# Tokens of a core pair split at 1152 instead of interleaved, with the first core's attention run two blocks ahead

## The reference, cut to what matters

```python
# B, T, C = 4, 2048, 2048; 16 heads of 128; hidden width 8192
xn = layernorm(x)
q, k, v = split(xn @ w_atten.T);  q, k = rope(q), rope(k)
att = softmax(where(causal, q @ k.T / sqrt(128), -inf))
s = (att @ v) @ w_proj.T
h = silu(xn @ w_gate) * (xn @ w_up)
h = keep_largest_2_of_4(h)          # by absolute value, in groups of four of the hidden width
g = silu(h @ w_down)
out = x + s * g
```

## Time and profile before

| | us |
|---|---|
| median of three runs | 2398.1 |
| the profiled execution, whole | 2320.1 |
| its span on the slowest core (5) | 2318.6 |
| spans of the eight cores | 2313.8 to 2318.6 |
| PE busy | 2233.9 (96%) |
| VectorE busy | 996.6 (43%) |
| ScalarE busy | 635.7 (27%) |
| the span in five stages, by PE's first and last matmuls | 126.0, 777.3, 110.5, 857.7, 447.1 |

### The profile page before, as it was taken

The page is one execution under the profiler, slowest core; times in us unless marked ns, Lnnn a source line. Parts: engine busy times, 40 slices in busy tenths (PEclk is TensorE's granted clock), DMA queues, the critical chain, the costliest instruction groups (busy, mean ns, idle before and its releaser), DMA issues.

```text
span 2318.6 us, 35747 instructions; the slowest of 8 cores (2313.8 to 2318.6 us)
## 1 busy us (share of the span) xinstructions
PE 2233.9 (96%) x12736; PEld 1181.9 (51%) x12736; DVE 996.6 (43%) x1441; ACT 635.7 (27%) x1082; POOL 137.5 (6%) x260
## 2 busy tenths in 40 slices
PE   4789999999999988999999999999999999999999
PEld 3547566675766744444444444444444444444444
DVE  5566867768677673004444443333333331000111
ACT  4624344444434434122222222222222200000000
POOL 0000000000000000000000000000000000000000
PEclk8999999999999999999999999999999999999999
DMA  9342322223122143754434344444554479766661
GB/s 268 109 79 47 61 40 45 57 44 66 38 46 56 33 79 74 156 111 80 83 74 73 73 80 83 90 94 91 97 101 94 91 168 238 157 127 132 132 138 44
DMA packets 82732, 217.38 MB, mean 94 GB/s; under 512 B 9984, under 2 KB 30592, under 8 KB 80000
## 3 DMA queue, kind: packets, MB, share of 16 engines
q0 software_dynamic: 36864, 134.23, 33.7%
q1 hardware_dynamic: 44576, 79.94, 11.0%
q10 hardware_dynamic: 1120, 0.92, 0.1%
HBM read 311.53 MB, written 25.17 MB: 145 GB/s over the span
## 4 chain that ended last, share of the span: by engine, by line
PE 82%; DVE 7%; issue 5%; DMA 3%; ACT 1%; DVEq 0%; ACTq 0%; SPq 0%
PE ps L554 37%; PE ps L573 19%; PE ps L432 8%; PE ps L443 7%; PE ps L539 5%; DVE arena L807 3%; DMA arena<-arena 2%; PE ps L520 2%; DVE arena L728 2%; PE ps L491 1%; PE ps L467 1%; DMA arena<-xN 1%; DVE arena L726 1%; PE ps L421 1%; DVE arena L738 1%
## 5 line engine op out<-in xcount | busy, mean ns | idle before, releaser
L554 PE MATMUL ps<-arena 128*128 128x512 bf16 x3968 | 856.6, 379 | 0.0
L554 PEld LDWEIGHTS ps<-arena 128*128 128x128 bf16 x3968 | 388.3, 98 | 468.1
L573 PE MATMUL ps<-arena 128*128 128x512 bf16 x2048 | 442.2, 379 | 1.1 <-DVE arena L858 1.1
L443 PE MATMUL ps<-arena 128*128 128x512 bf16 x1536 | 363.1, 385 | 14.2 <-ACT arena L630 14.2
L858 DVE TENSOR_TENSOR arena<-arena,ps 128x512 f32<-128x512 f32 x124 | 85.0, 685 | 633.7 <-PE ps L554 633.7
L573 PEld LDWEIGHTS ps<-arena 128*128 128x128 bf16 x2048 | 200.3, 98 | 242.9 <-issue 1.5
L432 PE MATMUL ps<-arena 128*128 128x256 bf16 x2048 | 241.1, 273 | 1.5 <-ACT arena L630 1.5
L443 PEld LDWEIGHTS ps<-arena 128*128 128x128 bf16 x1536 | 147.0, 99 | 167.6 <-issue 24.7
L696 ACT ACTIVATE arena<-arena 128x512 f32<-128x512 f32 x128 | 80.6, 630 | 519.5 <-DVE arena L858 519.5
L673 ACT ACTIVATE arena<-ps,arena 128x256 f32<-128x256 f32 (+7 forms) x128 | 156.4, 1222 | 230.9 <-DVE arena L811 230.8
L432 PEld LDWEIGHTS ps<-arena 128*128 128x128 bf16 x2048 | 197.1, 98 | 24.9 <-issue 1.8
(11 more groups left out here) (54 smaller groups left out, 1394.5 us busy)
## 6 DMA issues: line engine op xcount, KB each, us to landing
arena<-wgu POOLq DMA_DIRECT2D x128, 512.0 KB, 6.1
arena<-wd POOLq DMA_DIRECT2D x64, 512.0 KB, 5.8
arena<-wqkv POOLq DMA_DIRECT2D x48, 512.0 KB, 5.7
arena<-xN SPq DMA_DIRECT2D x16, 1024.0 KB, 12.7
arena<-arena SPq DMA_DIRECT2D x178, 64.0 KB, 2.1
arena<-wp POOLq DMA_DIRECT2D x16, 512.0 KB, 6.0
d_s<-arena SPq DMA_DIRECT2D x32, 256.0 KB, 4.0
d_hT<-arena SPq DMA_DIRECT2D x16, 512.0 KB, 6.7
```

The lines of the kernel that those rows point to most:

```text
L443: mm = e.matmul(bank[:], w[:, f, :], xnv[tile // 2][:, f, (tile % 2) * 512:(tile % 2 + 1) * 512], start=(f == 0), stop=(f == NF - 1))
L554: mm = e.matmul(ps[2 * p + up][:], w[:, f, :], xnv[0][:, f, half * 512:(half + 1) * 512], start=(f == 0), stop=(f == NF - 1))
L573: mm = e.matmul(ps[2 * (fc % 4) + half][:], w[:, j, :], hT[16 * q + j][:, half * 512:(half + 1) * 512], start=(q == 0 and j == 0), stop=(q ...
```

## The change

The two cores of a pair now own unequal, contiguous ranges: core 0 tokens 0 to 1151 (nine blocks), core 1 tokens 1152 to 2047 (seven blocks). The first core therefore needs only the keys and values of nine blocks; the second those of all sixteen. Both programs stand in the kernel, and each engine picks one by a flag that is loaded first. `Plan` holds each core's sizes and orders, `Buffers` its layout. Tiles of own tokens are 3 x 384 columns wide on the first core and 2 x 448 on the second; k tiles 384 and 448.

On both cores a block's values are now computed alone (128 columns), ScalarE copies the whole transposed block, and the mask is one block wide. Six banks instead of four take projections, and the fill pairs' activations (six pairs on the first core, four on the second) stand between the projection's copies. The first core also has alternate banks for the scores, the maximum of w ahead of the division of w-1 on VectorE, transposes and values of w-2 in window w, two buffers for the exponentials, a block order 0, 1, 4 to 7, 2, 3, 8, the projection begun between the last blocks, and a down order over two output blocks, with POOL's eighth down piece held until the reloads have landed.

```diff
+class Plan:
...
+    def __init__(self, p):
...
+        self.tok0 = 1152 * p
+        self.own = 896 if p else 1152
+        self.nb = self.own // 128
+        self.nw = H * self.nb
+        self.nln = 16 if p else 9
+        self.keys = 128 * self.nln
+        self.nt = 2 if p else 3
+        self.tw = self.own // self.nt
...
+        self.kt = [(i * 384, 384) for i in range(3)] + ([(1152, 448), (1600, 448)] if p else [])
+        self.vt = [list(range(2 * i, min(2 * i + 2, self.nln))) for i in range((self.nln + 1) // 2)]
+        self.ahead = p == 0
+        self.npe = 2 if self.ahead else 1
+        self.order = [0, 1, 4, 5, 6, 7, 2, 3, 8] if self.ahead else list(range(self.nb))
+        self.banks = [[0, 2, 0, 3, 0, 2, 0, 2, 0], [3, 0, 2, 0, 2, 0, 2, 0, 1]] if self.ahead else [[0] * self.nb] * 2
+        self.lag = 2 if self.ahead else 1
...
+        self.nfill = 2 * self.nt
+        self.nra = 6 if p else 7
+        self.nrb = 8 if p else 7
...
+        self.npair = 4 * NGB * self.nt
...
+        self.fcs = 4 if p else 2
...
+        self.down = [(fc, q) for fc in range(n) for q in (0, 1)] + [(fc, q) for q in (2, 3) for fc in range(n)]
+        self.down += [(fc, q) for fc in range(n, NF) for q in range(4)]
...
+    def windows(self):
...
+        want = [60 + self.blocks(w) if self.ahead else 27 + self.blocks(w) for w in range(self.nw)]
+        if self.p:
+            want = [x if w < self.nb * (H - 1) else 0.65 * x for w, x in enumerate(want)]
...
+            for share in ((0.5, 0.5) if self.ahead else (0.4, 0.6)):
...
+        def scores(w):
...
+            elif not P.ahead:
+                e.wait_ge(S["a_ex"], w)
+            elif w >= 2:
+                e.wait_ge(S["a_ex"], w - 1)
...
+        for w in range(P.nw):
+            scores(w)
+            if P.ahead:
+                if w >= 2:
+                    turn_p(w - 2)
+                steps(P.parts[w][0])
+                if w >= 2:
+                    values(w - 2)
             else:
+                if w >= 2:
+                    values(w - 2)
+                steps(P.parts[w][0])
+                if w:
+                    turn_p(w - 1)
+            steps(P.parts[w][1])
...
+        if P.ahead:
+            turn_p(P.nw - 2)
+            project(0)
+            values(P.nw - 2)
+            project(1)
+            turn_p(P.nw - 1)
+            project(2)
+        else:
+            values(P.nw - 2)
+            project(0)
+            turn_p(P.nw - 1)
+        values(P.nw - 1)
...
+        for k in range(16 * P.nt):
+            leave_s(k)
+            if k >= 6 and k % 2 == 0 and k // 2 - 3 < P.nfill:
+                activate(k // 2 - 3)
...
+        for w in range(P.nw + 1):
+            if P.ahead:
+                if w < P.nw:
+                    largest(w)
+                if w:
+                    divide(w - 1)
+            else:
+                if w:
+                    divide(w - 1)
+                if w < P.nw:
+                    largest(w)
+            if w >= P.lag:
+                for u in P.early[w - P.lag] + P.late[w - P.lag]:
+                    if u in P.rope_no:
+                        rope(P.rope_no[u])
...
+                    if P.ahead and b - 16 - NGU == P.nrb:
+                        for i in range(4):
+                            e.wait_ge(S[f"dHR{i}"], 16)
...
+    def by_core(e, prog):
+        e.wait_ge(S["dFL"], 16)
+        f = e.alloc_register("which_" + prog.__name__)
+        e.reg_load(f, flag[0:1, 0:1])
+        with e.If_eq(f, 0):
+            prog(e, PLANS[0], BUFFERS[0])
+        with e.Else():
+            prog(e, PLANS[1], BUFFERS[1])
+    def run_sync(e):
+        e.dma_start(out=flag[0:1, 0:1], in_=which[:]).then_inc(S["dFL"], 16)
+        by_core(e, prog_sync)
```

More of the change, by code:

```diff
@@ L66 @@
 ]
[L69 to L98, removed]
@@ L123 @@
[L123 to L145, removed]
@@ L148, in window_table @@
[L148 to L157, removed]
-        else:
[L159 to L165, removed]
-DOWN = [(fc, q) for fc in range(4) for q in (0, 1)] + [(fc, q) for fc in range(4) for q in (2, 3)]
@@ new lines, in prog_sync @@
+        for w in range(P.nw + 1):
+            for u in P.early[w] + P.late[w]:
+                if u in P.rope_no:
+                    swap(P.rope_no[u])
+        for k in range(16 * P.nt):
+            fc, t = P.proj[k]
+            e.wait_ge(S["a_se"], k + 1)
+            e.dma_start(out=d_s[fc * 128:(fc + 1) * 128, t * P.tw:(t + 1) * P.tw],
+                        in_=M.s_stage[k % 4][:]).then_inc(S[f"dS{k % 4}"], 16)
+        d_hTv = d_hT[:, 0:32 * P.own].rearrange("p (c x) -> p c x", x=P.own)
@@ new lines, in turn_p, with values @@
+            for k in range(n):
+                if k == 8 and w:
+                    e.wait_ge(S["a_y"], w)
+                mm = e.transpose(psT[:, k, :], M.pbf[w % P.npe][:, k * 128:(k + 1) * 128], M.id[:])
+            mm.then_inc(S["p_t"])
+        def values(w):
+            h, n = w // P.nb, P.blocks(w)
+            e.wait_ge(S["a_te"], w + 1)
+            if w:
+                e.wait_ge(S["a_y"], w)
+            e.wait_ge(S["a_u"], P.value_unit(w) + 1)
+            v = M.vg[(h // 2) % 2]
+            for k in range(n):
+                mm = e.matmul(ps[7][:, 0:128], v[:, k, (h % 2) * 128:(h % 2 + 1) * 128], M.pT[w % 2][:, k, :],
+                              start=(k == 0), stop=(k == n - 1))
@@ L496, in prog_tensor @@
         u = 0
-        for what in START:
+        for what in P.start:
             if what[0] == "x":
@@ new lines, in project @@
+        def project(k):
+            f, t = P.proj[k]
+            if t == 0:
+                wait_piece(e, P, NA + NFP + f)
+            if k >= 6:
+                e.wait_ge(S["a_se"], k - 5)
+            elif k < 2:
+                e.wait_ge(S["a_u"], len(P.units) - 1 + k)
+            else:
+                e.wait_ge(S["a_ex"], P.nw)
+            if k < 6:
+                last = max(w for w in range(P.nb) if P.block(w) * 128 < (t + 1) * P.tw)
+                e.wait_ge(S["a_y"], P.nw - P.nb + last + 1)
+            w = M.ringB[(NFP + f) % P.nrb][:].rearrange("p (c d) -> p c d", d=128)
@@ L579, in prog_tensor, with prog_scalar @@
                 mm.then_inc(S["p_dp"])
-    def prog_scalar(e):
+    def prog_scalar(e, P, M):
         def leave(u):
-            g, kind, h2, tile = UNITS[u]
+            g, kind, h2, t = P.units[u]
+            cols = P.matmuls(u)[1]
+            bank = ps[4 + u % 2]
             e.wait_ge(S["p_u"], u + 1)
             if kind in ("gate", "up"):
-                if u == NQKV:
-                    e.wait_ge(S["p_s"], 8 * (H - 1))
-                e.copy((graw if kind == "gate" else uraw)[g][:], ps[4 + u % 2][:]).then_inc(S["a_u"])
+                e.copy((M.graw if kind == "gate" else M.uraw)[g][:], bank[:, 0:cols]).then_inc(S["a_u"])
@@ L865, in prog_vector @@
+        for k in range(P.nt * NF):
             b = k % 3
```

1040 lines of the change are left out of this document (546 added, 494 removed).

## The result

The changed kernel takes 2285.3 us in the median of four runs (2221.8 to 2578.0), the kernel before, run beside it, 2360.9. These medians hold runs in which the cores of one die had a lower granted clock; the comparison leaves them out and gives **a ratio of 0.958 (95% interval 0.955 to 0.960): 4.2% faster**. The profiled execution took 2221.8 us, against 2320.1 before and 2196 forecast.

The account below looks back on a forecast made before the run. TensorE bounds the kernel, so matmul columns plus start and attention losses are counted. The first core decides: 3 + 72 + (506.9 + 15) + 124.6 + 967.1 + 498.6 + 3 + 4.5 = 2194.7, plus 1.5: 2196 us, range 2168 to 2262.

Parts of the forecast that it names:

- Rival E: First core's 11,520 matmuls of 384 columns cost more than their columns; at 181 ns each, 2411 us; chance 0.03.
- forecast case: Whole kernel ending between 2165 and 2220 us, around the forecast of 2196; chance 0.54.
- Rival A: First core's attention windows do not hide VectorE; 96 rotation windows lose 0.45 us each, 43 for 10: 2229; chance 0.13.
- Rival B: First core's alternating score banks fail; attention windows lose as before, 50 us instead of 15: 2231; chance 0.08.
- Rival D: Turn to down: reloads of h late by more than 10 us, 2206 to 2213; chance 0.07.
- Rival C: Second core ends last, its VectorE chain costing over 0.62 us a window; at 1.0, 2240; chance 0.12.
- Rival F: Second core's 1456 128-column value products wait for weight loads, 98 ns instead of 56, +61 us: 2224; chance 0.03.
- ScalarE needs per window ... under 2.9 of 3.52: First core's attention: ScalarE's exponential, block copy, unit and y copy take under 2.9 of a window's 3.52 us.
- PE's waits for exponentials under 3 us: Sign for the first core's attention stage: PE's exponential waits, 14.2 us before, fall under 3 us.
- 10 for VectorE: Part of the first core's 15 us attention charge: 10 us for VectorE running late in windows.
- 3 for the clock: Part of the first core's 15 us attention charge: 3 us for the low clock after the start.
- The end, 2 us: Part of the first core's 15 us charge: 2 us at the attention stage's end, otherwise filled by projection units.

Follow-up runs that it names:

- experiments one and two: Changed kernel with the first core's fill split 0.65 to 0.35 (one) or 0.35 to 0.65 (two) between transposes and values, instead of half and half: 0.950 and 0.971.
- experiment five: Kernel of experiment three (plain order, one set of score banks) with rotations two windows behind their unit instead of one: 0.963.
- experiment seven: Changed kernel with fill split 0.65 to 0.35 and the start's last two rotations moved behind the division of block 1: 0.947.
- experiment six: Changed kernel with rotations one window behind their unit instead of two, banks and order kept: 2276.6 and 2277.3 us, about 0.979.
- experiment three: Changed kernel with the plain order on the first core: one score buffer, blocks in order, one window of lag; tokens and held weights kept: 1.004.
- experiment nine: Changed kernel with the branch exchanged, so the second core's program comes first in the code: 0.958.
- experiment eleven: Changed kernel with fill split 0.8 to 0.2, start's last two rotations after block 1's division, and VectorE's division ahead of the reduction: 0.947.

## Why the prediction was right, and where its sum was off

**What held.** The forecast was a count of columns for the core that ends last, and that is what the time is. Gate and up took 969.9 us for 967.1 counted, down 500.6 (the stage less its tail) for 501.6, the price of 384 columns was right to 0.1 ns. Rival E is out. The start was 71.7 us with the flag, against 75. That is two errors against each other: the last tile landed at 52.4, the early end of my 52 to 62, but was transposed only at 62.1 to 63, since VectorE stood 3.4 us for a swap ahead of its statistics and did a rotation between them and the normalisation, and PE came to it behind a unit. The projection stage took 126.7 for 124.6; it now holds the last blocks' transposes and values, and 0.8 us of waits.

**What was luck.** The 2221.8 us lie 1.8 above the forecast case (2165 to 2220) and inside the stated range (2168 to 2262), whose upper part was there for rivals A, B and D and most of C and F. None of them came in the changed kernel; a cost that I had put at nothing took up their room. The 36.6 us lost in attention are nearer B's 50 than my 15.

**The step that failed: attention's losses on the first core, 15 us charged, 36.6 lost** (543.5 less 506.9). Point by point:

- *"ScalarE needs per window ... under 2.9 of 3.52."* From this the sum put ScalarE at nothing. It is a share of an engine, and as such true: ScalarE is busy 308.6 of 543.5 us. But PE needs the copy at a certain place, right after the fill between transposes and values, and only half of the window's fill stands before that place, while the copy of nine blocks takes 1.12 us and starts and is seen 0.3 us late at either end. The gaps were 22.4 us; experiments one and two show the cause by three doses. I had the copy's 1012 ns at 1024 columns and did not set it against the fill it must hide under.
- *"PE's waits for exponentials under 3 us"*: 6.4 us, in one wait. In every other window they are gone, but the alternating banks need not be the reason that I gave: experiment five has one set of banks and 1.2 us of such waits outside the start. This one is the start's: the reduction of the first scores stands behind the rotation of k2, whose swap landed late. Mended in experiment seven, worth 7 us with the low clock after it (granted clock 0.56 of full between 83.5 and 87.0 us, after PE had been idle for 6 us, so mostly the lower of the two levels).
- *"10 for VectorE"*: 7.4 us ahead of the transposes. *"3 for the clock"*: the stretch above lost about 1.5 us.
- *The end, 2 us*: 0.8.

**Rival A** did not come in the changed kernel (7.4 us of gaps ahead of the transposes, where it asked for 43), but it is what the kernel becomes without the second window of lag: 42.2 us of waits for divisions on core 0 in experiment six, 61.3 on core 6 in experiment three. I had counted that second window only as an argument against A ("the swap has two windows to land"). It is worth 54 us with the rest of the order in place and 90 without; the rest is worth 19 with it and 55 without.

**Rival B** (the alternating banks bring nothing, 2231): its sign did not come, since the exponential waits of before are gone but for the start's. But the banks were not run apart, and by experiment five they may bring little. Experiment three does not settle it: it drops the second window too, and is slower than the changed kernel by 4.8% and than B's figure by 100 us, since I priced B by the losses of before per window; VectorE's waits for swaps rose instead from 47.7 us to 105.1.

**Rival C**: the second core's swap waits are 29.5 us over 112 rotations, against 47.7 over 96 before. It loses 0.18 us a window where C needed 0.62, and where I had charged 0.31.

**Rival D**: no wait for h at all, 3 us charged. The reloads were issued 13.4 us into down, and POOL, which waits for all four, goes on 41.6 us into it: 28 us for four, 7 each, where I had estimated 8 and the last at 48.

**Rival F**: the value products run at 56 ns on core 0 (the timeline at 385.70), and core 1's stage leaves no room for more: 1456 products at 98 instead of 56 ns would be 61 us and it loses 19.8 in all. The 81 ns of the page that I cited (the Trainium skill, TensorE: Matmul & The Clock Gate, Back-to-back issue gap) would have cost 74 us by my estimate, and no stretch here shows it.

**The tail**: 7.9 for 4.5. 3.2 of the 3.4 us are the jump at the end of the first arm (experiment nine), which I had put into a flag's price at the head alone. The first core jumps at the end, the second at the head; the 3 us of the flag on the first core were 2.9 for the DMA, the load and the branch not taken.

Sum of the deviations of the first core: start -3.3, attention +21.6, projection +2.1, gate and up +2.8, down -1.0, tail +3.4: +25.6, which is 2196 against 2221.8.

**Open:** what the banks, the blocks' order, the split of the fill and the two exponentials are worth each by itself; and what the last 13 us of attention losses in experiment eleven (520.3 less 506.9) would take, since each repair after the first was followed by gaps at another step.

## What to carry to other kernels

An engine whose share of a window is well below one can still stop the bound engine in every window, when its result is needed at a fixed place: set the duration of each step on the chain between two instructions of the bound engine against the work that stands between them, not against the window. When an engine's queue holds a step that waits for a DMA, everything behind it inherits the wait, so a second window of lead for a small transfer was worth more here than the reordering of the compute (54 and 19 us, each with the other in place). And when the matmuls of a stage get shorter, check again what hid under them; here this was not tested by itself.

## What the runs showed of the hardware that was not expected

- A taken branch at the head of the program costs 3.7 us on core 0 (6.64 less 2.92) and 4.1 on core 1 (7.12 less 2.98), and jumping over the other arm at the end 3 to 4 us (7.9 and 4.7, 9.1 and 5.0).
- The swap of a rotation usually lands before it is asked for in the changed kernel (VectorE waits for 6 of 96), but the waits reach 7.3 us, and 6.9 with the plain order. The 7.3 us stand beside a weight piece of 512 KB: between 71.7 and 77.9 us POOL's queue took 0.83 of the time of the 16 DMA engines, the queue of the swap 0.06.
- Matmuls of 128 columns, each with new weights, start 56 ns apart in runs of nine, though one weight load is recorded at 98 ns.
